# Six of sixteen products with B of a state-space scan moved from VectorE to GpSimd, each released by a node's row-maxima scores

## The chip, the cores and the metric

One core of a Trainium2 chip runs the whole program. The metric is the device time of one execution in microseconds (us); the time before is the median of three runs.

## What is computed

Sixteen sequences of 128 rows and 256 features go through three stages, each added to or replacing the stream:

```
x = x + mamba(layernorm(x))        # h_t = exp(dt*A) * h_{t-1} + (dt*u) * B_t ;  y_t = sum_n h_t[n] * C_t[n]
x = x + mlstm(layernorm(x), ctx)   # four heads, gates, normalised heads
x = x + ffn(layernorm(x))          # six nodes, each: q, k, v projections, softmax attention of 8 heads, Wo, + q
```

In the first stage the state has 512 channels times 16 components per sequence. `(dt*u) * B` is the inflow of the scan; it is the product that the change is about.

## The kernel before

The sequences are taken in eight groups of two (`NG`, `GB`). All engines walk one list, `ORDER`: every step of every stage has a slot in it, a group's FFN (`"f"`) has 67 slots, and the steps of the scan (`"u"`), of its input part (`"a"`) and of the mLSTM (`"x"`) of later groups are put between them by hand-written tables of slots. While the FFN of group g runs, VectorE also does the second half of the scan of group g+1, the mLSTM of group g+1, the input part of group g+2 and the first part of the scan of group g+2. Engines run their own steps strictly in the order of the list and wait for each other on semaphores.

The scan of a group is cut into sixteen units k (`UNITS`), each a tile of 128 partitions by 1024 values in one of three ring buffers (`ring`, unit k in buffer `(16*i+k) % 3`). A unit goes through five steps: ScalarE makes the decays (`dec`, L844, four activations); VectorE makes the inflow, `feed` (L1064): ring = dtus * bs, the product with B; VectorE runs the recurrence in place, `scan` (L1071); VectorE multiplies with C, `weigh` (L1080); TensorE folds the components together, `add` (L535), which frees the buffer (semaphore `ysum`). In the list `feed` of unit k+1 stands ahead of `scan` of unit k. After four units `gather` (L1088, L1090) closes a channel block.

In the FFN each node c (0 to 5) does: q, k and v projections (L632, L613, L642); the scores of all eight heads into a four-bank PSUM tile `heads` (L663, semaphore `smax_ps`); the row maxima of these by VectorE into `mx` (L1171, step `("f","max",c)`); a transpose of `mx` (L668) and the scores again with the maxima taken off (L671, L676); the exponentials (ScalarE L917); values and denominators (L688, L690); the division in two halves by VectorE (L1180, step `attend`); the output projection (L710). "Row maxima" below means L1171, and "ready" the end of the L663 in front of it. The first tensor that L710 needs is the first half of `aT`, its last four matmuls need the second half.

Until the change GpSimd clears some buffers at the start and issues a few transfers; then it has nothing to do. The SyncE queue fills `bs`, `cs`, `dts`, `dtus`, and waits there for the semaphores `inflow` (products done) and `outflow`.

Of the kernel before, what the change touches and what calls it, by code (L numbers as in the profile page):

```python
# [7 lines left out]
ALU = mybir.AluOpType  # L8
# [3 lines left out]
P = 128  # L12
B, L, H = 16, 128, 256
GB = 2
T = GB * L
NG = B // GB
# [21 lines left out]
RING = 3  # L38
STEPS = GB * HC


# [72 lines left out]
for _rank, (_name, _steps, _at, _shift) in enumerate(AT):  # L114
# [7 lines left out]
        -236, -227, -227, -194, -155, -146, -82]  # L122
ORDER += [(at, 5, 0, n, step) for n, (step, at) in enumerate(zip(W_STEPS, W_AT))]
ORDER = [(step, g) for _, _, g, _, step in sorted(ORDER)]

# [39 lines left out]

PRE = ["c0_tail", "dt_c0", "dtu_c0", "pool_warm", "dt_first", "dtu_first", "stats_seen", "in_loaded", "alog_loaded", "win_loaded", "wing_loaded", "wx_loaded", "const_loaded", "pool_consts", "pool_zeros", "vec_consts", "prep_ps", "prep_read",
       "prep_vec", "prep_bias_ps", "prep_bias", "w_loaded", "w_used", "setup_act", "gate_sum"]


def build(nc, x, ctx_in, consts, vecs, rowvecs, w_in, w_x, w_dt, w_out, w_gate, w_edge, w_edgeT, w_node, out):  # L170
    bc_rows = nc.dram_tensor("bc_rows", (2, 2, NS, T), F32, kind="Internal").ap()
    dt_rows = nc.dram_tensor("dt_rows", (2, 2, IC, SD, BLKS, T), F32, kind="Internal").ap()
    with ExitStack() as es:
# [110 lines left out]
        def after(eng, name, i, n):  # L284

            value = i * PER[name] + n
            if value > 0:
                eng.wait_ge(sig[name], value)

        def walk(steps):  # L290

            for (kind, name, n), group in ORDER:
                if kind + name in steps:
                    steps[kind + name](group, n)
# [31 lines left out]
        def _(sp):  # L326
# [62 lines left out]
            def spread_rows(i, q):  # L389

                after(sp, "bc_stored", i, 32)
                for j, (dst, name, used) in enumerate(((bs, "bs_in", "inflow"), (cs, "cs_in", "outflow"))):
                    after(sp, used, i - 1, UNITS - CUNITS + q + 1)
                    rows_of = bc_rows[i % 2, j].rearrange("(n g) t -> g n t", g=NGRP)[q]
                    sp.dma_start(dst[:, q, :], rows_of.partition_broadcast(SD)
                                 ).then_inc(sig[f"{name}{q}"], 16)

            def chunk(i, c):
                if i == 0 and c == 0:
                    return  # L400

                for j, (dst, name, used) in enumerate(((dts, "dt", "decay"), (dtus, "dtu", "inflow"))):
                    after(sp, f"{name}_stored", i, 16 * BLKS)
                    after(sp, used, i, (c - 1) * CUNITS)
                    sp.dma_start(dst[c % 2][:].rearrange("p k t -> p (k t)"),
# [544 lines left out]
        def _(dve):  # L950
# [103 lines left out]
            def feed(i, k):  # L1054

                c, q = k // CUNITS, k % CUNITS
                if q == 0:
                    if i == 0 and c == 0:
                        dve.wait_ge(sig["dtu_first"], 16 * BLKS)
                    after(dve, f"dtu_in{c % 2}", i, 16 * (c // 2 + c % 2))  # L1060
                if c == 0:
                    after(dve, f"bs_in{q}", i, 16)
                after(dve, "ysum", i, k - RING + 1)
# [3 lines left out]
            def scan(i, k):  # L1067
                states = ring[(i * UNITS + k) % RING][:].rearrange("p k t -> p (k t)")
                after(dve, "decay", i, k + 1)
                after(dve, "inflow", i, k + 1)  # L1070
                v.tensor_tensor_scan(states, dec[k % 2][:].rearrange("p k b t -> p (k b t)"), states, 0.0, ALU.mult,  # L1071
# [63 lines left out]
            def head_norm(i, _):  # L1135
# [20 lines left out]
                scale = rowv[:, 0:1, :].rearrange("p o (h d) -> p o h d", h=XH)  # L1156
                m_chain.link(v.tensor_tensor(hb, hb, scale.broadcast_to([P, GB, XH, XD]), ALU.mult))

            def mlstm_out(i, step):
                if step == 1:  # L1160
                    return
                xi = xr[i % 2]
                heads_of = xi[:].rearrange("p b (h d) -> p b h d", h=XH)
# [50 lines left out]
        def _(pool):  # L1214
# [15 lines left out]
            first_chunk(pool, dtus, dtu, "dtu")  # L1230


# [63 lines left out]
```

## Time and profile before

| | |
|---|---|
| three runs | 1228.12, 1223.46 and 1228.3 us; median 1228.12 |
| profiled execution | span 1224.7 us, first to last instruction; no time of its own is listed, and the median stands 3.4 us above this span |
| TensorE | busy 1102.9 us, 90% of the span |
| VectorE | busy 980.0 us, 80% |
| ScalarE | busy 733.8 us, 60% |
| GpSimd | busy 15.2 us, all before 47 us |
| mean granted TensorE clock | 0.939 of full speed |

The page gives busy time per engine, the groups of instructions with the idle time in front of them and what ended it, and the chain of work that ended last. The timeline gives single instructions, and in square brackets how long the engine was idle before one and which instruction released it. An instruction on VectorE can be shown to start up to 0.1 us before the end of the one before.

### The profile page before, as it was taken

To read this page: it belongs to the slowest core of one execution; us is meant where nothing else is said; L and a number is where in the kernel's file an instruction comes from. 1 tells how busy PE (TensorE), PEld (TensorE's weight loads), DVE (VectorE), ACT (ScalarE), POOL (GpSimd) and SP (SyncE) were. 2 spreads that over 40 slices of the span, in tenths; PEclk is the share of its full clock that TensorE was granted. 3 is DMA by queue.
4 is the path that set the end of the run, shared out by engine and by line. 5 is a ranking of instruction groups with operands and counts; after the bars stand their busy time and mean duration, and the time that the engine had idled before them with its cause. 6 is when DMAs were issued, how large, how long until landed. Compare 5 with 4: busy or idle time off the path is not lost.

```text
span 1224.7 us, 27095 instructions
## 1 busy us (share of the span) xinstructions
PE 1102.9 (90%) x11540; PEld 842.8 (69%) x11540; DVE 980.0 (80%) x1219; ACT 733.8 (60%) x1728; POOL 15.2 (1%) x32
## 2 busy tenths in 40 slices
PE   8866779999999998999899989999999988998886
PEld 6743456767777676777677767777777766776775
DVE  2398978799998998999999989999988989635122
ACT  3535442776577665776587657765676656544443
POOL 4000000000000000000000000000000000000000
PEclk9777686999999999999999999999999999999998
DMA  6631523013110412041112201041104120000000
GB/s 203 204 115 58 161 93 120 36 36 106 44 62 11 131 36 70 7 134 36 36 37 82 86 17 61 17 124 45 52 11 131 35 62 1 2 2 10 2 1 10
DMA packets 52791, 76.08 MB, mean 62 GB/s; under 512 B 13696, under 2 KB 37504, under 8 KB 52672
## 3 DMA queue, kind: packets, MB, share of 16 engines
q1 hardware_dynamic: 51968, 73.81, 19.2%
q8 instruction: 90, 1.47, 0.5%
q0 software_dynamic: 704, 0.56, 0.2%
q14 instruction: 29, 0.24, 0.1%
HBM read 62.55 MB, written 10.75 MB: 60 GB/s over the span
## 4 chain that ended last, share of the span: by engine, by line
PE 62%; DVE 10%; ACT 8%; issue 3%; DVEq 0%; ACTq 0%
PE ps L632 7%; PE heads L642 7%; PE ps L710 6%; PE ps L703 5%; PE ps L613 5%; PE heads L663 4%; PE heads L671 4%; PE ps L535 4%; PE ps L502 3%; DVE mx L1171 3%; PE ps L559 2%; PE ps L688 2%; PE heads L688 1%; PE heads L613 1%; PE ps L690 1%
## 5 line engine op out<-in xcount | busy, mean ns | idle before, releaser
L1071 DVE TENSOR_TENSOR_SCAN ring<-dec,ring 128x1024 f32<-128x1024 f32 x128 | 292.0, 2281 | 1.7 <-ACT dec L844 1.2
L844 ACT ACTIVATE dec<-dts,a_neg 128x254 f32<-128x254 f32 x512 | 220.0, 500 | 16.8 <-DVE ring L1071 16.7
L1171 DVE TENSOR_REDUCE mx<-heads 128x16 f32<-128x2048 f32 x48 | 109.7, 2286 | 65.3 <-PE heads L663 64.7
L1080 DVE TENSOR_TENSOR ring<-ring,cs 128x1024 f32<-128x1024 f32 x128 | 156.0, 1218 | 1.9
L1064 DVE TENSOR_TENSOR ring<-dtus,bs 128x1024 f32<-128x1024 f32 x128 | 155.1, 1217 | 2.3 <-PE ps L535 1.8
L917 ACT ACTIVATE pr<-heads 128x512 f32<-128x512 f32 x192 | 99.1, 603 | 41.3 <-PE heads L676 41.3
L535 PE MATMUL ps<-ring,fold 128*32 128x256 f32 x1024 | 88.6, 416 | 26.3 <-DVE ring L1080 26.2
L710 PE MATMUL ps<-aT,wo_f 128*128 128x256 f32 x384 | 94.1, 387 | 8.0 <-DVE aT L1180 8.0
L703 PE MATMUL ps<-node,we_f 128*128 128x256 f32 x384 | 99.2, 403 | 0.0
L632 PE MATMUL ps<-node,wq_f 128*128 128x256 f32 x384 | 94.9, 390 | 3.4 <-ACT node L932 3.4
L642 PE MATMUL heads<-wv_f,node 128*128 128x256 f32 x384 | 94.1, 388 | 0.0
L632 PEld LDWEIGHTS ps<-node,wq_f 128*128 128x128 f32 x384 | 69.8, 190 | 27.2 <-ACT node L932 18.5
L710 PEld LDWEIGHTS ps<-aT,wo_f 128*128 128x128 f32 x384 | 70.1, 190 | 25.5 <-DVE aT L1180 17.2
L613 PE MATMUL ps<-node,wk_f 128*128 128x256 f32 x320 | 83.1, 405 | 0.0
L703 PEld LDWEIGHTS ps<-node,we_f 128*128 128x128 f32 x384 | 74.0, 200 | 13.2 <-issue 2.4
L642 PEld LDWEIGHTS heads<-wv_f,node 128*128 128x128 f32 x384 | 70.4, 190 | 17.3 <-issue 9.1
L897 ACT ACTIVATE qT<-ps,fb 128x256 f32<-128x256 f32 x96 | 40.2, 470 | 56.4 <-PE ps L632 55.4
L663 PE MATMUL heads<-kT,qT 32*128 32x128 f32 x1536 | 57.9, 288 | 16.7 <-ACT qT L897 11.9
L502 PE MATMUL ps<-th,win 128*128 128x256 f32 x256 | 65.4, 401 | 8.0 <-ACT u L777 5.8
L613 PEld LDWEIGHTS ps<-node,wk_f 128*128 128x128 f32 x320 | 60.0, 198 | 18.3 <-issue 9.3
L663 PEld LDWEIGHTS heads<-kT,qT 32*128 32x128 f32 x1536 | 49.5, 190 | 30.0 <-issue 30.0
L932 ACT ACTIVATE node<-ps,fb 128x256 f32<-128x256 f32 x96 | 40.1, 468 | 43.1 <-PE ps L710 43.1
(183 smaller groups left out, 1753.5 us busy)
## 6 DMA issues: line engine op xcount, KB each, us to landing
dts<-dt_rows SPq DMA_DIRECT2D x31, 512.0 KB, 3.9
dtus<-dt_rows SPq DMA_DIRECT2D x31, 512.0 KB, 5.1
node<-in_w_edgeT SPq DMA_DIRECT2D x18, 256.0 KB, 3.1
bs<-bc_rows SPq DMA_DIRECT2D x32, 128.0 KB, 5.0
cs<-bc_rows SPq DMA_DIRECT2D x32, 128.0 KB, 5.1
dt_rows<-dt SPq DMA_DIRECT2D x32, 128.0 KB, 2.4
dt_rows<-th SPq DMA_DIRECT2D x32, 128.0 KB, 2.5
xin<-in_x SPq DMA_DIRECT2D x8, 256.0 KB, 3.1
```

The costliest lines, as they stand in the source:

```text
L535: last = mm(MY[SD * blk:SD * (blk + 1), 0:T], fold[:], ring[(i * UNITS + k) % RING][:, blk, :], start=(q == 0), stop=(q == NGRP - 1), tile ...
L613: last = mm(bank[:, a * T:(a + 1) * T], w[:, k, a * P:(a + 1) * P], src[:, k, :], start=(k == 0), stop=(k == HC - 1))
L632: last = mm(FA[:, a * T:(a + 1) * T], wq_f[c][:, k, a * P:(a + 1) * P], src[:, k, :], start=(a == 0 and k == 0), stop=(k == HC - 1), skip_ ...
L642: last = mm(X3[:, b * H:(b + 1) * H], node[SLOT[GRAPH[c]["v"]]][:, k, b * L:(b + 1) * L], wv_f[c][:, k, :], start=(k == 0), stop=(k == HC ...
L663: last = mm(heads[:, h, to], qT[at], kT[c % 2][at], start=True, stop=True, tile_position=(FD * h, 0))
L703: mm(ED[:, a * T:(a + 1) * T], we_f[c][:, k, a * P:(a + 1) * P], src[:, k, :], start=(a == 0 and k == 0), stop=False, skip_group_check=True)
L710: last = mm(ED[:, a * T:(a + 1) * T], wo_f[c][:, k, a * P:(a + 1) * P], aT[:, k, :], start=False, stop=(k == HC - 1), skip_group_check=True)
L844: last = fn(dec[k % 2][:, blk, :, 1:L], dts[c % 2][:, blk, :].rearrange("p (b t) -> p b t", b=GB)[:, :, 1:L], ACT.Exp, scale=a_neg[:, c, b ...
L1064: v.tensor_tensor(ring[(i * UNITS + k) % RING][:], dtus[c % 2][:], bs[:, q:q + 1, :].broadcast_to([P, BLKS, T]), ALU.mult).then_inc(sig["i ...
L1071: v.tensor_tensor_scan(states, dec[k % 2][:].rearrange("p k b t -> p (k b t)"), states, 0.0, ALU.mult, ALU.add).then_inc(sig["state"], 1)
L1080: v.tensor_tensor(states[:], states[:], cs[:, q:q + 1, :].broadcast_to([P, BLKS, T]), ALU.mult).then_inc(sig["outflow"], 1)
L1171: v.tensor_reduce(mx[:].rearrange("p (h s) -> p h s", h=HPC)[:, :, 0:STEPS], heads[:].rearrange("p h (s k) -> p h s k", s=STEPS), AX.X, AL ...
```

## The change

`POOL_FED` names, for each group, the units whose product GpSimd makes: none in group 0, units 8, 11 and 14 in group 1, and 2, 4, 6, 8, 11 and 14 in groups 2 to 7, 39 in all. VectorE skips these. GpSimd's new step stands in the list directly behind a row maximum (`POOL_AT`), and waits for the scores of that node (`smax_ps`), for its inputs and for the ring buffer. Its products count in a semaphore of their own, `pool_fed`, and whoever waited for the count of products now waits for both (`wait_fed`). Steps of all other engines stay in their slots. Besides, the last product of `head_norm` is only marked, and what reads it waits for it one step later.

```diff
+POOL_FED = ((), (8, 11, 14)) + ((2, 4, 6, 8, 11, 14),) * (NG - 2)
...
+POOL_AT = [(2, -30.95), (4, -19.95), (6, -8.95), (8, 3.05), (11, 14.05), (14, 25.05)]
+ORDER += [(FSLOTS * (g - 1) + at, 6, g, k, ("u", "pfeed", k)) for g in range(1, NG) for k, at in POOL_AT if k in POOL_FED[g]]
...
+        def wait_fed(eng, i, n):
+
+            mine = sum(UNITS - len(POOL_FED[g]) for g in range(i)) + len([k for k in range(n) if k not in POOL_FED[i]])
+            pools = sum(len(POOL_FED[g]) for g in range(i)) + len([k for k in POOL_FED[i] if k < n])
+            if mine:
+                eng.wait_ge(sig["inflow"], mine)
+            if pools:
+                eng.wait_ge(sig["pool_fed"], pools)
...
             def feed(i, k):
 
                 c, q = k // CUNITS, k % CUNITS
-                if q == 0:
-                    if i == 0 and c == 0:
-                        dve.wait_ge(sig["dtu_first"], 16 * BLKS)
-                    after(dve, f"dtu_in{c % 2}", i, 16 * (c // 2 + c % 2))
-                if c == 0:
-                    after(dve, f"bs_in{q}", i, 16)
+                if k in POOL_FED[i]:
+                    return
+                if i == 0 and c == 0:
+                    dve.wait_ge(sig["dtu_first"], 16 * BLKS)
+                after(dve, f"dtu_in{c % 2}", i, 16 * (c // 2 + c % 2))
+                after(dve, f"bs_in{q}", i, 16)
...
             def scan(i, k):
                 states = ring[(i * UNITS + k) % RING][:].rearrange("p k t -> p (k t)")
                 after(dve, "decay", i, k + 1)
-                after(dve, "inflow", i, k + 1)
+                wait_fed(dve, i, k + 1)
...
-                m_chain.link(v.tensor_tensor(hb, hb, scale.broadcast_to([P, GB, XH, XD]), ALU.mult))
+                m_chain.mark(v.tensor_tensor(hb, hb, scale.broadcast_to([P, GB, XH, XD]), ALU.mult))
 
             def mlstm_out(i, step):
                 if step == 1:
                     return
+                m_chain.wait(m_chain.n)
...
+            def feed(i, k):
+
+                c, q = k // CUNITS, k % CUNITS
+                if k not in POOL_FED[i]:
+                    return
+                grp, node_c = [(grp, step[2]) for step, grp in ORDER[:ORDER.index((("u", "pfeed", k), i))]
+                               if step[:2] == ("f", "max")][-1]
+                after(pool, "smax_ps", grp, node_c + 1)
+                after(pool, f"dtu_in{c % 2}", i, 16 * (c // 2 + c % 2))
+                after(pool, f"bs_in{q}", i, 16)
+                after(pool, "ysum", i, k - RING + 1)
+                g.tensor_tensor(ring[(i * UNITS + k) % RING][:], dtus[c % 2][:],
+                                bs[:, q:q + 1, :].broadcast_to([P, BLKS, T]), ALU.mult).then_inc(sig["pool_fed"], 1)
+
+            walk(dict(upfeed=feed))
```

VectorE around the row maxima of node 2 in the FFN of group 3, before: L1064 is `feed`, the two products shown are those of units 14 and 15 of group 4.

```order
L1090 TENSOR_TENSOR gate1<-gate1,u1 128x256
L1080 TENSOR_TENSOR ring2<-ring2,cs 128x1024
L1064 TENSOR_TENSOR ring1<-dtus1,bs 128x1024
L1171 TENSOR_REDUCE mx<-heads 128x4x4
L1071 SCALAR_TENSOR_TENSOR ring0<-dec1,ring0 128x1024
L1047 SCALAR_TENSOR_TENSOR dt<-dt,th 128x1024
L1050 TENSOR_TENSOR th<-dt,u0 128x1024
L1080 TENSOR_TENSOR ring0<-ring0,cs 128x1024
L1064 TENSOR_TENSOR ring2<-dtus1,bs 128x1024
L1071 SCALAR_TENSOR_TENSOR ring1<-dec0,ring1 128x1024
L1180 TENSOR_TENSOR aT<-ps3,aT 128x256
```

The same place after the change; line numbers have moved: `feed` is L1082, `scan` L1089, `weigh` L1098, row maxima L1190, `attend` L1199.

```order
L1108 TENSOR_TENSOR gate1<-gate1,u1 128x256
L1098 TENSOR_TENSOR ring2<-ring2,cs 128x1024
L1190 TENSOR_REDUCE mx<-heads 128x4x4
L1089 SCALAR_TENSOR_TENSOR ring0<-dec1,ring0 128x1024
L1065 SCALAR_TENSOR_TENSOR dt<-dt,th 128x1024
L1068 TENSOR_TENSOR th<-dt,u0 128x1024
L1098 TENSOR_TENSOR ring0<-ring0,cs 128x1024
L1082 TENSOR_TENSOR ring2<-dtus1,bs 128x1024
L1089 SCALAR_TENSOR_TENSOR ring1<-dec0,ring1 128x1024
L1199 TENSOR_TENSOR aT<-ps3,aT 128x256
```

Only the product of unit 14, directly ahead of the row maxima, is gone; everything behind them is as it was.

GpSimd's stream for group 4, units 2, 4, 6, 8, 11 and 14 with their waits (`bs_in` and `dtu_in` are the inputs' transfers); it has nothing else between them:

```order
L1262 TENSOR_TENSOR ring0<-dtus0,bs 128x1024 [waits bs_in2,ysum,dtu_in0,smax_ps]
L1262 TENSOR_TENSOR ring2<-dtus1,bs 128x1024 [waits bs_in0,ysum,dtu_in1,smax_ps]
L1262 TENSOR_TENSOR ring1<-dtus1,bs 128x1024 [waits bs_in2,ysum,dtu_in1,smax_ps]
L1262 TENSOR_TENSOR ring0<-dtus0,bs 128x1024 [waits bs_in0,ysum,dtu_in0,smax_ps]
L1262 TENSOR_TENSOR ring0<-dtus0,bs 128x1024 [waits bs_in3,ysum,dtu_in0,smax_ps]
L1262 TENSOR_TENSOR ring0<-dtus1,bs 128x1024 [waits bs_in2,ysum,dtu_in1,smax_ps]
```

Each is one instruction of 1024 values per partition, and none was on GpSimd before. The first three are behind the scores of nodes 3 to 5 of FFN 2, the last three behind nodes 0 to 2 of FFN 3.

VectorE around the row maxima of node 0 in the FFN of group 6 (units 7 and 8 of group 7), before and then after:

```order
L1064 TENSOR_TENSOR ring2<-dtus1,bs 128x1024 [waits ysum]
L1071 SCALAR_TENSOR_TENSOR ring1<-dec0,ring1 128x1024 [waits inflow,decay]
L1080 TENSOR_TENSOR ring1<-ring1,cs 128x1024 [waits state]
L1064 TENSOR_TENSOR ring0<-dtus0,bs 128x1024 [waits ysum,dtu_in0]
L1171 TENSOR_REDUCE mx<-heads 128x4x4 [waits smax_ps]
L1071 SCALAR_TENSOR_TENSOR ring2<-dec1,ring2 128x1024 [waits inflow,decay]
L1080 TENSOR_TENSOR ring2<-ring2,cs 128x1024 [waits state]
L1064 TENSOR_TENSOR ring1<-dtus0,bs 128x1024 [waits ysum]
L1071 SCALAR_TENSOR_TENSOR ring0<-dec0,ring0 128x1024 [waits inflow,decay]
```

```order
L1082 TENSOR_TENSOR ring2<-dtus1,bs 128x1024 [waits ysum,bs_in3,dtu_in1]
L1089 SCALAR_TENSOR_TENSOR ring1<-dec0,ring1 128x1024 [waits pool_fed,inflow,decay]
L1098 TENSOR_TENSOR ring1<-ring1,cs 128x1024 [waits state]
L1190 TENSOR_REDUCE mx<-heads 128x4x4 [waits smax_ps]
L1089 SCALAR_TENSOR_TENSOR ring2<-dec1,ring2 128x1024 [waits pool_fed,inflow,decay]
L1098 TENSOR_TENSOR ring2<-ring2,cs 128x1024 [waits state]
L1082 TENSOR_TENSOR ring1<-dtus0,bs 128x1024 [waits ysum,bs_in1,dtu_in0]
L1089 SCALAR_TENSOR_TENSOR ring0<-dec0,ring0 128x1024 [waits pool_fed,inflow,decay]
```

The product into `ring0` (unit 8) is gone from in front of the row maxima, and the recurrences now also wait for GpSimd's count.

## Rows read from the trace of the kernel before

**Rows 1.** Busy time of each engine in two stretches (start:end, length, busy, instructions, granted clock).

```profile
590.00:720.00 130.00, 122.58 (x1392) 94.14 (x1391) 120.40 (x147) 89.37 (x213) 0.00 (x0) 0.99 0.19 58
982.00:1102.00 120.00, 108.97 (x1306) 84.07 (x1306) 84.86 (x106) 65.63 (x163) 0.00 (x0) 0.99 0.06 17
```

**Rows 2.** Page, part 5: the product with B on VectorE.

```profile
L1064 DVE TENSOR_TENSOR ring<-dtus,bs 128x1024 f32<-128x1024 f32 x128 | 155.1, 1217 | 2.3 <-PE ps L535 1.8
```

**Rows 3.** GpSimd's instructions, grouped by line and form (busy us, mean ns).

```profile
L1220 POOL MEMSET dec<- 128x1024 f32 x2 | 1.8, 951 | 0.0
...
L1216 POOL MEMSET ones<- 128x128 f32 x1 | 0.2, 204 | 0.3 <-POOLq L1289 0.3
```

**Rows 4.** Timeline of all engines, 43.8 to 45.5 us.

```profile
43.89 0.42 DVE L1045 TENSOR_TENSOR th<-dt,u 128x256 f32<-128x256 f32 x1
...
44.61 1.08 POOL L322 DMA_DIRECT2D dtus<-th  x2 [31.05 <-DVE th L1045]
```

**Rows 5.** Timeline of VectorE, 600 to 735 us (start, length, instruction, idle before).

```profile
629.37 0.42 DVE L1180 TENSOR_TENSOR aT<-ps,aT 128x256 f32<-128x256 f32 x1 [0.95 <-ACT aT L927]
...
648.55 0.41 DVE L1180 TENSOR_TENSOR aT<-heads,aT 128x256 f32<-128x256 f32 x1
...
657.46 2.29 DVE L1171 TENSOR_REDUCE mx<-heads 128x16 f32<-128x2048 f32 x1 [2.07 <-PE heads L663]
659.67 2.28 DVE L1071 TENSOR_TENSOR_SCAN ring<-dec,ring 128x1024 f32<-128x1024 f32 x1
...
670.16 0.42 DVE L1180 TENSOR_TENSOR aT<-heads,aT 128x256 f32<-128x256 f32 x1
...
676.33 2.29 DVE L1171 TENSOR_REDUCE mx<-heads 128x16 f32<-128x2048 f32 x1
...
679.04 0.42 DVE L1090 TENSOR_TENSOR gate<-gate,u 128x256 f32<-128x256 f32 x1
...
684.09 0.69 DVE L1102 TENSOR_TENSOR xr<-xr,ps 128x512 f32<-128x512 f32 x1 [0.15 <-PE ps L559]
```

**Rows 6.** Timeline of TensorE, 600 to 735 us.

```profile
648.17 1.98 PE L710 MATMUL ps<-aT,wo_f 128*128 128x256 f32 x8
...
655.83 1.58 PE L663 MATMUL heads<-kT,qT 32*128 32x128 f32 x32
...
669.99 1.89 PE L710 MATMUL ps<-aT,wo_f 128*128 128x256 f32 x8
...
676.20 0.64 PE L535 MATMUL ps<-ring,fold 128*32 128x256 f32 x8
```

**Rows 7.** Timeline of TensorE, in the groups of 264 us and of 786 us.

```profile
278.19 2.05 PE L710 MATMUL ps<-aT,wo_f 128*128 128x256 f32 x8
...
801.45 1.13 PE L710 MATMUL ps<-aT,wo_f 128*128 128x256 f32 x4 [0.17 <-DVE aT L1180]
```

**Rows 8.** Timeline of VectorE, 264 to 287 us.

```profile
278.63 0.42 DVE L1180 TENSOR_TENSOR aT<-heads,aT 128x256 f32<-128x256 f32 x1
```

**Rows 9.** Timeline of VectorE, 984 to 1060 us.

```profile
1004.28 1.22 DVE L1064 TENSOR_TENSOR ring<-dtus,bs 128x1024 f32<-128x1024 f32 x1
1005.41 2.28 DVE L1171 TENSOR_REDUCE mx<-heads 128x16 f32<-128x2048 f32 x1
```

**Rows 10.** Timeline of TensorE, 984 to 1130 us.

```profile
1003.19 1.18 PE L663 MATMUL heads<-kT,qT 32*128 32x128 f32 x32 [0.73 <-issue]
...
1007.75 0.33 PE L668 MATMUL ps<-cst,mx 128*128 128x128 f32 x1 [0.77 <-DVE mx L1171]
...
1015.71 1.99 PE L710 MATMUL ps<-aT,wo_f 128*128 128x256 f32 x8 [1.99 <-DVE aT L1180]
...
1043.51 0.33 PE L668 MATMUL ps<-cst,mx 128*128 128x128 f32 x1 [0.63 <-DVE mx L1171]
...
1126.20 0.33 PE L668 MATMUL ps<-cst,mx 128*128 128x128 f32 x1 [0.48 <-DVE mx L1171]
```

**Rows 11.** Who waited for whom, whole run (us in total, times, longest).

```profile
PE ps L668 <- DVE mx L1171: 6.2, 8, 2.4
```

More of the change, by code:

```diff
@@ L164 @@
 )
-PRE = ["c0_tail", "dt_c0", "dtu_c0", "pool_warm", "dt_first", "dtu_first", "stats_seen", "in_loaded", "alog_loaded", "win_loaded", "wing_loaded", "wx_loaded", "const_loaded", "pool_consts", "pool_zeros", "vec_consts", "prep_ps", "prep_read",
+PRE = ["pool_fed", "c0_tail", "dt_c0", "dtu_c0", "pool_warm", "dt_first", "dtu_first", "stats_seen", "in_loaded", "alog_loaded", "win_loaded", "wing_loaded", "wx_loaded", "const_loaded", "pool_consts", "pool_zeros", "vec_consts", "prep_ps", "prep_read",
        "prep_vec", "prep_bias_ps", "prep_bias", "w_loaded", "w_used", "setup_act", "gate_sum"]
@@ L391, in spread_rows @@
                 after(sp, "bc_stored", i, 32)
-                for j, (dst, name, used) in enumerate(((bs, "bs_in", "inflow"), (cs, "cs_in", "outflow"))):
-                    after(sp, used, i - 1, UNITS - CUNITS + q + 1)
+                for j, (dst, name) in enumerate(((bs, "bs_in"), (cs, "cs_in"))):
+                    if j:
+                        after(sp, "outflow", i - 1, UNITS - CUNITS + q + 1)
+                    elif i:
+                        wait_fed(sp, i - 1, UNITS - CUNITS + q + 1)
                     rows_of = bc_rows[i % 2, j].rearrange("(n g) t -> g n t", g=NGRP)[q]
@@ L400, in chunk @@
                     return
-                for j, (dst, name, used) in enumerate(((dts, "dt", "decay"), (dtus, "dtu", "inflow"))):
+                for j, (dst, name) in enumerate(((dts, "dt"), (dtus, "dtu"))):
                     after(sp, f"{name}_stored", i, 16 * BLKS)
-                    after(sp, used, i, (c - 1) * CUNITS)
+                    if j:
+                        wait_fed(sp, i - (c < 1), (c - 1) * CUNITS if c else UNITS - CUNITS)
+                    else:
+                        after(sp, "decay", i, (c - 1) * CUNITS)
                     sp.dma_start(dst[c % 2][:].rearrange("p k t -> p (k t)"),
```

## The prediction

> **What bounds the kernel now.** I began with the busy time by stretch. In a middle group TensorE is busy 122.58 of 130 us and VectorE 120.40; in the stretch that holds the last scan steps VectorE has fallen to 84.86 of 120 and TensorE to 108.97 [rows 1]. Both engines look full in the middle, so the busy share does not say which one pays. The timelines do. The row maxima of node 2 were preceded by 2.07 us in which VectorE stood idle until the scores were there [rows 5]: VectorE reaches this point early, and what it does ahead of the row maxima is covered. Behind them it is the other way round. It runs without a pause through the recurrence and what follows, and the second half of `aT` is finished when TensorE comes to it, or just after. So a group is a chain of stretches from one node's scores to the next; ahead of the scores VectorE has time to spare, and behind them it has almost none in some nodes. The exception is FFN 6, where the input part of a later group is missing from TensorE's work: there VectorE comes late to two row maxima and TensorE waits for it, 0.77 and 0.63 us at L668 and 1.99 us at L710 [rows 10].
>
> **What is removed.** 39 products of 1.217 us [rows 2], 47.5 us of VectorE's 980. Which of them stood on the path? Units 8, 11 and 14 were made ahead of the row maxima of nodes 0, 1 and 2, unit 6 ahead of node 5, unit 2 between nodes 3 and 4, unit 4 just behind node 4. In FFN 0 to 5 the scores end TensorE's stretch and VectorE is there in time or in the last instruction before, and TensorE does not wait for `mx`. Earlier arrival brings nothing: gain 0. What covers it is TensorE's own work of the stretch; without that cover each would be worth 1.13 us, the distance from one product's start to the next instruction (1004.28 to 1005.41 [rows 9]). In FFN 6 there is a gain:
> - Node 0: scores end at 1003.19 + 1.18 = 1004.37 [rows 10], the row maxima start at 1005.41, behind the product of unit 8 [rows 9]. Without it they start 0.06 after the scores, as at node 2 of group 3 (657.41 to 657.46), so 0.98 earlier. What is behind them, up to the wait of 1.99 us at L710, comes forward by this.
> - Node 1: no gain. Node 2: the product of unit 14 goes, and with it TensorE's 0.63 us [rows 10].
> Together 0.98 + 0.63 = 1.6 us, if nothing is given back.
>
> **What is added: 39 products on GpSimd.** The trace has no elementwise product on GpSimd. Its nearest rows are the clearing of a 128x1024 tile in 0.951 us and of a 128x128 tile in 0.204 [rows 3], 0.83 ns for a value and 0.10 us fixed. A product reads two values and writes one. If the write is hidden behind the reads it takes 2 x 0.83 x 1.024 + 0.10 = 1.81 us; if all three take turns, 2.66. I take the middle, 2.24 us. GpSimd started 0.30 us after the VectorE instruction that released it (43.89 + 0.42 to 44.61 [rows 4]). So a product ends 0.30 + 2.24 = 2.54 us after the scores.
>
> The Trainium skill (GPSIMD Engine Reference, "Performance versus the Vector engine") gives 4497 ns for an addition of 2048 fp32 values and advises VectorE for such work. With the fixed 0.10 us that makes, as an estimate, 2.30 us here, and the total below would be 2.7 us instead of 1.6. No row here shows it.
>
> Is anybody waiting for that end? The users of the products are not: the recurrence that reads unit 8 stands behind the row maxima, another recurrence, a weighing, six convolution steps and another product; unit 11 has two products and recurrences in front of it, and so on. The SyncE queue doesn't either: what refills `bs` behind unit 14 stands in its queue behind a transfer that waits for the weighing of unit 13, which is later. The 39 products cost VectorE only if the two engines are in each other's way when both read operands from SBUF. During the row maxima they are not, since these read PSUM. The instruction behind them (a recurrence) reads two SBUF tensors. No row shows the two at work together. The lower bound of the cost is nothing; the upper bound is that this instruction waits until the product is done. I take the upper bound with the middle product, because it is also near the middle of all combinations. The recurrence stood 659.67 - 657.41 = 2.26 us behind the scores [rows 5, 6]. So the overhang is 2.54 - 2.26 = 0.28 us. What each stretch makes of it, in FFN 0 to 5:
> - Node 0: VectorE waited 0.95 us for ScalarE ahead of `aT` [rows 5]. The overhang disappears: 0.
> - Node 1: the second half of `aT` was done at 648.55 + 0.41 = 648.96 [rows 5]; L710 needs it halfway through, 648.17 + 0.99 = 649.16 [rows 6]. With the 0.04 us from one to the other, 0.16 to spare: cost 0.12, six times, 0.7 us.
> - Node 2: in FFN 0 the half was done at 279.05 [rows 8] and needed at 278.19 + 0.95 = 279.14 [rows 7], 0.05 to spare: 0.23, and I count FFN 1 and 5 like it: 0.69. In FFN 4 TensorE already waited 0.17 us for it [rows 7]: 0.28 in full. In FFN 2 and 3 the half was done at 670.58 [rows 5], needed at 669.99 + 0.95 = 670.94 [rows 6]: 0. Sum 1.0 us.
> - Node 3: unit 2 needs the ring buffer of the unit 15 before, which TensorE frees at 676.20 + 0.64 = 676.84 [rows 6], after the scores. The product ends at 676.84 + 0.30 + 2.24 = 679.38. The next instruction with two SBUF tensors is the gate at 679.04 [rows 5], so 0.34 late; ahead of L1102, where VectorE waited 0.15 [rows 5], 0.19 is left, six times 1.1 us.
> - Nodes 4 and 5: at node 4 VectorE was still in a recurrence when the scores came, is free now, and is ahead by that much; at node 5 nothing with two large SBUF operands follows within reach. 0.
> That is 2.8 us. In FFN 6 the overhang takes 0.28 of the 0.98 at node 0 and 0.12 at node 1; the gain there is 0.70 - 0.12 + 0.63 = 1.2. The moved wait of the mLSTM norm can let `aT` start some 0.08 us earlier, the amount by which the recurrence at 659.67 starts before the row maxima's end [rows 5]; under 1 us in all, and nothing where ScalarE is the later one. I count it 0. More waits stand on VectorE's products and recurrences; they are met long before and are taken up while the instruction ahead runs: 0.
>
> **Sum.** +2.8 - 1.2 = +1.6 us on the profiled execution's 1224.7. Its surroundings, 3.4 us to the median, are the same in both kernels. 1228.12 + 1.6 = 1229.7 us, +0.13%. About 0.5%, 6.1 us, is what a measurement of this kernel can tell from no change.
>
> **Ends.** Nothing given back (a product of 1.81 us, or no hindrance): -1.6, 1226.5 us. A product of 2.66 us makes an overhang of 0.70: node 1 3.2, node 2 1.95 + 0.70 + 0.68 = 3.3, node 3 0.61 x 6 = 3.7, and FFN 6 gains only 0.28 - 0.54 + 0.63 = 0.4: +9.8, 1237.9 us. Between 0.28 and 0.70 each 0.1 us of overhang costs 2.0 us, so 6.1 us is passed at 0.51, a product of 2.47 us.
>
> **Rivals.**
> - *The overhang becomes the bound* (slower): the product takes 2.47 us or more and VectorE stands still behind every row maximum of nodes 1 to 3. For it: node 2 has no time to spare in any view, and the upper bound from the clearing rows allows it. Against it: the middle of the bounds doesn't reach it. 1234 to 1238 us, chance 0.20.
> - *The product catches the operands first* (slower): if GpSimd is released while VectorE still has an instruction with two SBUF operands to start ahead of the row maxima, `mx` itself is 2.24 us later, straight on TensorE's path. Decides from three such meetings a run. Against it: before the change at most one instruction was under way at the scores, and 0.30 us to wake leaves it to finish. Chance 0.04. The Trainium skill (SBUF — State Buffer, "Who interferes with whom") says that a VectorE instruction with two SBUF inputs and a GpSimd instruction that reads SBUF exclude each other for their whole length, by order of issue; by that rule both rivals' mechanism exists, and their price depends on who comes first; no row here shows it.
> - *No hindrance* (the change does its work and nobody needed it): 1226.5 us, chance 0.14.
> - *TensorE's waits for the row maxima vanish as a whole* (faster): 6.2 us over the run, eight waits [rows 11], would give 1221.9 us. Against it: two of the eight are in FFN 6 and counted; others stand in FFN 7 (0.48 at 1126.20 [rows 10]), which has no scan beside it. Chance 0.05.
> - The forecast, overhang 0.1 to 0.5: chance 0.57.
>
> Faster by over 0.5%: 0.06. Within: 0.57 + 0.14 = 0.71 less a little for the sum of small errors, 0.70. Slower: 0.24. The range takes the no-hindrance end and most of the long product, with the scatter of the runs shown (1223.46 to 1228.3) below: 1224 to 1236.5.
>
> **What would show it.** GpSimd's busy time rises to about 39 x 2.24 + 15 = 103 us; a product's length beside the row maxima decides the sum. The start of the recurrence behind the row maxima: 2.26 us after the scores without hindrance, 2.5 by my sum, more in the rival. VectorE's busy time falls by 47 us and its idle time ahead of row maxima grows by about as much. TensorE's 0.77 and 0.63 us at L668 in FFN 6 are gone, the 1.99 at L710 is about 1.3. In FFN 4 the wait of 0.17 us in the middle of L710 becomes 0.45. I am wrong if a product takes far from 2.2 us, if VectorE's other instructions get longer beside it, or if the row maxima do.

## The result: slower by 0.85%

The kernel with the change takes 1237.29 us, the median of 13 runs (1228.36 to 1241.91); the kernel before took 1227.42 us in 13 runs (1221.03 to 1230.5). The ratio is 1.0085, with a 95% interval of 1.0062 to 1.0108, so it is slower, and the whole interval lies above the half per cent that the prediction took as the least difference it could tell. The forecast of 1229.7 us was wrong, and the median lies 0.8 us above the range. The profiled execution took 1241.91 us, its span 1240.1 us, where that of before was 1224.7: 15.4 us to explain. (The median of the runs moved less, 9.9 us; the profiled one is the slowest of the thirteen.) "Kernel 1" to "kernel 7" below mean the kernels of experiments 1 to 7.

The page of the kernel with the change, busy time by engine and two groups of its costliest instructions (busy us, mean ns, then idle time before them and what ended it). Lines have moved by 18 or 19: L1064 is now L1082, L1071 is L1089, L1090 is L1108, L1171 is L1190, L663 is L681.

```profile
PE 1106.7 (89%) x11540; PEld 841.8 (68%) x11540; DVE 950.5 (77%) x1180; ACT 732.6 (59%) x1728; POOL 110.8 (9%) x71
...
L1262 POOL TENSOR_TENSOR ring<-dtus,bs 128x1024 f32<-128x1024 f32 x39 | 95.6, 2450 | 917.4 <-PE heads L681 796.9
...
L1082 DVE TENSOR_TENSOR ring<-dtus,bs 128x1024 f32<-128x1024 f32 x89 | 112.0, 1266 | 2.5 <-PE ps L553 2.0
```

GpSimd does 39 products in 95.6 us, 2450 ns each, and VectorE is left with 89 of 128. But the mean of VectorE's own products, 1217 ns in [rows 2], has risen to 1266: some of them stood still. Next, GpSimd's waits over the whole run (us in total, times, longest), and then the lengths of its products (minimum/median/maximum in ns):

```profile
POOL ring L1262 <- PE heads L681: 796.9, 33, 177.9
POOL ring L1262 <- DMA bs<-bc_rows: 120.5, 6, 21.1
```

The products' line:

```profile
L1262 POOL TENSOR_TENSOR ring<-dtus,bs x39: 2344/2359/3253, 223.5 to 1056.2; 128x1024 f32<-128x1024 f32 x39
```

33 products waited for the scores, as the change intends. Six waited for a transfer of `bs`. One product a group in six groups is exactly unit 2, and this wait is in no term of the prediction.

Where the 15.4 us are is found by the distance from one node's scores to the next, as in the prediction's stretches. From node 3 to node 4 it was 22.77, 23.12, 22.73, 23.09, 22.76 and 22.73 us in FFN 0 to 5; it is 24.70, 26.27, 26.33, 24.67, 24.66 and 26.02. That is 15.45 us more, the whole loss. In FFN 0 to 5 node 0 to 1 stays 21.98, node 4 to 5 stays 20.43, node 1 to 2 goes from 18.97 to 19.03 and node 2 to 3 from 18.76 to 18.83 where the granted clock is 1.00 in both. What else differs goes with that clock (from node 5 of FFN 2 to node 0 of FFN 3 it is 26.57 us at 1.00 before, 28.02 at 0.94 now; behind FFN 0 27.57 at 0.94 before, 26.45 at 1.00 now), up to 1.5 us either way. All the other distances, the start and the end together cancel to 0.05 us in these two executions.

The stretch behind node 3 in FFN 3, first SyncE's queue (a row is a transfer's issue), then GpSimd, VectorE and TensorE, all from timelines of the kernel with the change:

```profile
670.09 2.82 SPq L390 DMA_DIRECT2D dt_rows<-dt  x4
672.95 1.90 SPq L394 DMA_DIRECT2D dt_rows<-th  x4
...
677.70 0.54 SPq L410 DMA_DIRECT2D bs<-bc_rows  x1
...
680.29 0.54 SPq L410 DMA_DIRECT2D bs<-bc_rows  x1
```

GpSimd in the same stretch:

```profile
685.91 2.35 POOL L1262 TENSOR_TENSOR ring<-dtus,bs 128x1024 f32<-128x1024 f32 x1 [19.12 <-DMA bs<-bc_rows]
```

VectorE in the same stretch:

```profile
683.25 2.28 DVE L1190 TENSOR_REDUCE mx<-heads 128x16 f32<-128x2048 f32 x1
...
685.95 2.59 DVE L1108 TENSOR_TENSOR gate<-gate,u 128x256 f32<-128x256 f32 x1
```

TensorE in the same stretch:

```profile
681.98 1.17 PE L681 MATMUL heads<-kT,qT 32*128 32x128 f32 x32 [0.66 <-ACT qT L915]
683.08 0.64 PE L553 MATMUL ps<-ring,fold 128*32 128x256 f32 x8
...
688.69 3.69 PE L577 MATMUL ps<-wout,gate 128*128 128x256 f32 x16 [1.45 <-DVE gate L1108]
...
696.08 0.66 PE L498 MATMUL ps<-cst,hrow 128*128 128x128 f32 x4 [0.47 <-DVE hrow L1023]
```

The scores of node 3 end at 681.98 + 1.17 = 683.15. The ring buffer is free at 683.08 + 0.64 = 683.72, 0.57 us behind the scores, as I had it. But the rows of B that unit 2 reads are issued at 680.29, behind eight stores of `dt` and `dt`*u, the chunk's own loads and the row group before, and the product starts at 685.91, 5.6 us later. By then VectorE has finished the row maxima, which read PSUM, and is at the gate (L1108), which reads two tensors in SBUF. The gate takes 2.59 us where it took 0.42 in [rows 5]: it is stalled for 2.17 us. TensorE waits 1.45 us for it at L577 and 0.47 us for `hrow` later, 1.92 us together. In the kernel before, the same transfer was issued at 673.18, also too late for an early product (the row maxima started at 676.33 [rows 5]), but VectorE made unit 2 only at 688.61. SyncE's queue in the kernel before:

```profile
673.18 0.55 SPq L395 DMA_DIRECT2D bs<-bc_rows  x1
```

And VectorE's timeline there:

```profile
688.61 1.22 DVE L1064 TENSOR_TENSOR ring<-dtus,bs 128x1024 f32<-128x1024 f32 x1
```

In the six groups the product of unit 2 starts 2.79, 4.43, 4.26, 2.76, 4.47 and 3.39 us behind the scores. Whatever VectorE has in hand with two SBUF operands then pays: the gate in FFN 0 and 3, the products of units 0 and 1 in FFN 2 and 5, the first recurrence in FFN 1 and 4. VectorE's timeline in FFN 2 and FFN 4, kernel with the change:

```profile
551.67 4.54 DVE L1082 TENSOR_TENSOR ring<-dtus,bs 128x1024 f32<-128x1024 f32 x2
...
821.54 4.44 DVE L1089 TENSOR_TENSOR_SCAN ring<-dec,ring 128x1024 f32<-128x1024 f32 x1
```

GpSimd's timeline in FFN 4:

```profile
820.59 3.25 POOL L1262 TENSOR_TENSOR ring<-dtus,bs 128x1024 f32<-128x1024 f32 x1 [20.82 <-DMA bs<-bc_rows]
```

The pair of products takes 4.54 us instead of 2.35, the recurrence 4.44 instead of 2.28: 2.19 and 2.16 us, the same stall as at the gate. In FFN 4 GpSimd came while VectorE was in a product with two SBUF operands (until 821.62); its own product is listed with 3.25 us because it waited as well.

The stall costs 1.9 us on the path wherever it falls, and in three of the six stretches 1.3 to 1.6 us more. Windows of the kernel with the change over the stretches of FFN 2 and 3 and over short pieces in FFN 2 (start:end, length, busy time and instructions of TensorE, its weight loads, VectorE, ScalarE and GpSimd, granted clock, DMA share, GB/s):

```profile
548.00:575.00 27.00, 24.71 (x262) 17.44 (x255) 23.50 (x29) 15.72 (x41) 2.40 (x2) 0.94 0.14 53
683.00:708.00 25.00, 22.77 (x249) 16.69 (x243) 23.13 (x29) 15.46 (x40) 2.42 (x2) 1.00 0.12 43
558.00:560.00 2.00, 1.50 (x48) 1.23 (x48) 1.82 (x5) 0.00 (x0) 0.00 (x0) 1.00 0.00 0
560.00:562.00 2.00, 0.53 (x4) 0.42 (x4) 1.49 (x5) 1.10 (x4) 0.00 (x0) 1.00 0.00 0
562.00:564.00 2.00, 2.00 (x27) 0.82 (x26) 2.00 (x2) 1.75 (x5) 0.00 (x0) 0.69 0.00 0
564.00:566.00 2.00, 2.00 (x6) 0.89 (x5) 2.00 (x4) 1.24 (x4) 0.00 (x0) 0.50 0.00 0
```

In FFN 2 the granted clock falls between 562 and 564 us and is 0.50, TensorE's lower level of 1.2 GHz, from 564 to 566. Before it TensorE had been busy only 1.50 and 0.53 us of two stretches of 2 us: it had waited 1.97 us in one piece for `hrow`. In FFN 3 the same 1.9 us are taken in two pieces, 1.45 and 0.47, and the clock stays at 1.00. FFN 4 shows that one piece doesn't always do it: TensorE waits 1.94 us there, and the clock stays at 1.00. TensorE's timeline at the two places:

```profile
561.47 0.66 PE L498 MATMUL ps<-cst,hrow 128*128 128x128 f32 x4 [1.97 <-DVE hrow L1023]
...
829.04 0.66 PE L498 MATMUL ps<-cst,hrow 128*128 128x128 f32 x4 [1.94 <-DVE hrow L1023]
```

So the sum is 6 x 1.92 = 11.5 us of stalls, 4.6 us of low clock, less 0.6 us that FFN 1 and 3 lost in the kernel before and don't now (23.12 and 23.09, where the rest show 22.7 to 22.8: TensorE waited 0.40 us for `hrow` in both): 15.5, where 15.45 was measured.

### The profile page after: what moved, and what is told of

Its sections match the earlier page's. It is cut to its first block and busy times, and to the rows that moved or that the text cites. A ratio compares the mean times of both kernels' runs of the same rounds, so it can differ in the third digit from the quotient of the medians.

```text
span 1240.1 us, 27202 instructions
## 1 busy us (share of the span) xinstructions
PE 1106.7 (89%) x11540; PEld 841.8 (68%) x11540; DVE 950.5 (77%) x1180; ACT 732.6 (59%) x1728; POOL 110.8 (9%) x71
## 5 line engine op out<-in xcount | busy, mean ns | idle before, releaser
L1089 DVE TENSOR_TENSOR_SCAN ring<-dec,ring 128x1024 f32<-128x1024 f32 x128 | 297.8, 2327 | 1.7 <-ACT dec L862 1.1
L1262 POOL TENSOR_TENSOR ring<-dtus,bs 128x1024 f32<-128x1024 f32 x39 | 95.6, 2450 | 917.4 <-PE heads L681 796.9
L1190 DVE TENSOR_REDUCE mx<-heads 128x16 f32<-128x2048 f32 x48 | 109.7, 2286 | 76.3 <-PE heads L681 75.7
L1098 DVE TENSOR_TENSOR ring<-ring,cs 128x1024 f32<-128x1024 f32 x128 | 156.1, 1219 | 1.9
L1082 DVE TENSOR_TENSOR ring<-dtus,bs 128x1024 f32<-128x1024 f32 x89 | 112.0, 1266 | 2.5 <-PE ps L553 2.0
L728 PE MATMUL ps<-aT,wo_f 128*128 128x256 f32 x384 | 96.0, 391 | 10.4 <-DVE aT L1199 10.3
L728 PEld LDWEIGHTS ps<-aT,wo_f 128*128 128x128 f32 x384 | 70.5, 191 | 29.0 <-DVE aT L1199 20.1
L681 PE MATMUL heads<-kT,qT 32*128 32x128 f32 x1536 | 57.0, 284 | 16.7 <-ACT qT L915 12.0
L681 PEld LDWEIGHTS heads<-kT,qT 32*128 32x128 f32 x1536 | 48.7, 187 | 30.0 <-issue 30.0
```

The source lines that it names most:

```text
L681: last = mm(heads[:, h, to], qT[at], kT[c % 2][at], start=True, stop=True, tile_position=(FD * h, 0))
L728: last = mm(ED[:, a * T:(a + 1) * T], wo_f[c][:, k, a * P:(a + 1) * P], aT[:, k, :], start=False, stop=(k == HC - 1), skip_group_check=True)
L1082: v.tensor_tensor(ring[(i * UNITS + k) % RING][:], dtus[c % 2][:], bs[:, q:q + 1, :].broadcast_to([P, BLKS, T]), ALU.mult).then_inc(sig["i ...
L1098: v.tensor_tensor(states[:], states[:], cs[:, q:q + 1, :].broadcast_to([P, BLKS, T]), ALU.mult).then_inc(sig["outflow"], 1)
L1190: v.tensor_reduce(mx[:].rearrange("p (h s) -> p h s", h=HPC)[:, :, 0:STEPS], heads[:].rearrange("p h (s k) -> p h s k", s=STEPS), AX.X, AL ...
```

## Experiments

**1. Is it unit 2?** All products as changed, but unit 2 back on VectorE.

```
-POOL_FED = ((), (8, 11, 14)) + ((2, 4, 6, 8, 11, 14),) * (NG - 2)
+POOL_FED = ((), (8, 11, 14)) + ((4, 6, 8, 11, 14),) * (NG - 2)
```

> The change without unit 2: GpSimd makes 8, 11 and 14 in group 1 and 4, 6, 8, 11 and 14 in groups 2 to 7; VectorE makes unit 2 again. Theory L (unit 2's product starts only when its row of B has landed, 2.7 us or more behind the scores of node 3, and then shuts VectorE out of its next instruction with two SBUF operands): the distance from the scores of node 3 to those of node 4 is 22.7 to 23.1 us again in all six groups, and the time is that of the kernel before or a little less, ratio to before 0.998 to 1.001. Theory O (the overhang behind every row maximum is the cost): unit 2 is one of six, ratio still 1.006 to 1.008.

Measured: 1225.07 us (1223.04 to 1234.34, 12 runs), ratio to the kernel before 0.999 (0.9967 to 1.0014). The distance from node 3 to node 4 is 22.78, 22.77, 22.75, 22.79, 22.78 and 22.74 us. VectorE behind the row maxima of node 3 in FFN 3:

```profile
678.68 0.43 DVE L1108 TENSOR_TENSOR gate<-gate,u 128x256 f32<-128x256 f32 x1
679.02 2.36 DVE L1082 TENSOR_TENSOR ring<-dtus,bs 128x1024 f32<-128x1024 f32 x2
```

The gate is at 0.43 and the two products at 2.36. The loss is gone, and the other 33 products cost nothing that can be measured. Nor does the moved wait of `head_norm`, which this kernel has too.

**2. Is unit 2 enough?** Only unit 2 on GpSimd, in the same six groups.

```
-POOL_FED = ((), (8, 11, 14)) + ((2, 4, 6, 8, 11, 14),) * (NG - 2)
+POOL_FED = ((), ()) + ((2,),) * (NG - 2)
```

> Only unit 2 of groups 2 to 7 on GpSimd, six products in all, all others on VectorE as before. Theory L: nearly the whole loss, ratio to before 1.008 to 1.012. Theory O: a sixth of it, ratio 1.001 to 1.003.

Measured: 1238.33 us (1234.1 to 1243.64, 6 runs), ratio 1.0077 (1.0046 to 1.0108), the whole loss of the change from six of its 39 products, though just under the 1.008 that was expected at least. Distances 24.69, 24.69, 24.68, 24.68, 24.68 and 26.28. Timelines of VectorE and GpSimd in FFN 3, and the windows of FFN 4 and 5:

```profile
681.49 0.42 DVE L1108 TENSOR_TENSOR gate<-gate,u 128x256 f32<-128x256 f32 x1
681.83 4.52 DVE L1082 TENSOR_TENSOR ring<-dtus,bs 128x1024 f32<-128x1024 f32 x2
```

GpSimd:

```profile
682.70 2.57 POOL L1262 TENSOR_TENSOR ring<-dtus,bs 128x1024 f32<-128x1024 f32 x1 [130.30 <-DMA bs<-bc_rows]
```

The windows, with the columns as above:

```profile
811.00:836.00 25.00, 22.73 (x261) 16.77 (x256) 23.12 (x29) 15.39 (x39) 2.44 (x1) 1.00 0.15 57
943.00:970.00 27.00, 24.72 (x256) 17.49 (x251) 23.09 (x27) 15.47 (x40) 3.22 (x1) 0.94 0.14 52
```

Five stretches lose 1.9 us at a clock of 1.00; the sixth loses 3.5, and its clock is 0.94. The five separate the stall, 1.92 us, from the clock, 1.6 us. In kernels 1, 3 and 4, where TensorE has no such wait behind node 3, the clock is 1.00 in all eighteen of these stretches.

**3. Is it the time at which the rows of B land?** All 39 products on GpSimd, as in the change, but on SyncE's queue the second and third of the four row groups of B (the third is the one that unit 2 reads) stand right behind the first, ahead of the stores of `dt`. The main lines of the edit:

```
+                order = [(0, q), (1, q)]
+                if i:
+                    order = {0: [(0, 0), (1, 0), (0, 1), (0, 2)], 1: [(1, 1)], 2: [(1, 2)], 3: [(0, 3), (1, 3)]}[q]
+                for j, r in order:
```

> All 39 products on GpSimd as in the change; in the SyncE queue of groups 1 to 7 the transfers of the second and third row group of B stand right behind the first row group's, ahead of the stores and reads of dt, so that they don't wait for them. Theory L: the product of unit 2 starts 0.6 to 0.8 us behind the scores of node 3 (when TensorE has freed its buffer), ends just behind the start of the gate, and the time falls to that of the kernel before or below, ratio to before 0.998 to 1.002. If instead a product of unit 2 at this place costs its time wherever its transfer lands, or if theory O holds: ratio 1.006 to 1.010.

Measured: 1225.09 us (1222.77 to 1232.15, 12 runs), ratio 0.9986 (0.9961 to 1.0011); every distance from node 3 to 4 is between 22.73 and 22.78. The timelines of GpSimd and VectorE in FFN 3:

```profile
675.50 2.37 POOL L1266 TENSOR_TENSOR ring<-dtus,bs 128x1024 f32<-128x1024 f32 x1 [17.12 <-PE ps L557]
```

VectorE:

```profile
677.54 0.61 DVE L1112 TENSOR_TENSOR gate<-gate,u 128x256 f32<-128x256 f32 x1
```

The product now waits for TensorE to free the ring buffer (L557 is the L535 of before), starts 0.77 us behind the scores and ends at 677.87. The gate takes 0.61 us instead of 0.42: late by 0.19, of which 0.15 disappear in the time that VectorE had ahead of the L1102 of the kernel before (`xr`). Same products, same engine, and the median is 12.2 us below that of the change (the two were measured apart; the ratios, each to the kernel before measured beside it, are 0.9986 and 1.0085, which is the same difference): the cause is the time of the transfer. Against the kernel before it is no gain that can be told from nothing.

**4. What do the two engines exclude each other by?** In place of unit 2's product GpSimd clears the ring buffer three times in a row. Each clearing writes as much as the product, and none reads anything; the inflow of unit 2 is then left out of the result.

```
+                if k == 2:
+                    tile_k = ring[(i * UNITS + k) % RING][:].rearrange("p k t -> p (k t)")
+                    for n in range(2):
+                        g.memset(tile_k, 0.0).then_inc(sig["pool_part"], 1)
...
+                    g.memset(tile_k, 0.0).then_inc(sig["pool_fed"], 1)
+                    return
```

> As the change, with the product of unit 2 replaced by three fills of the same tile with zero, one after the other (about 3 us of GpSimd, released by the same waits): GpSimd writes there and reads nothing, so unit 2's inflow is zero. If GpSimd and VectorE exclude each other only where both read SBUF operands: the gate keeps its 0.42 us and the two products behind it 2.35 us, node 3 to node 4 is 22.7 to 23.1 us, ratio to before 0.998 to 1.002. If any work of GpSimd on SBUF, or the wait for its count, is what holds VectorE: gate or products are stretched as in the change, ratio 1.006 to 1.012.

Measured: 1224.9 us (1221.79 to 1233.1, 12 runs), ratio 0.9971 (0.9951 to 0.9991), a little below the 0.998 to 1.002 that was expected. GpSimd and VectorE in FFN 3:

```profile
676.16 1.96 POOL L1265 MEMSET ring<- 128x1024 f32 x2 [18.87 <-DMA bs<-bc_rows]
678.17 0.95 POOL L1267 MEMSET ring<- 128x1024 f32 x1
```

VectorE:

```profile
676.46 0.42 DVE L1108 TENSOR_TENSOR gate<-gate,u 128x256 f32<-128x256 f32 x1
676.81 2.35 DVE L1082 TENSOR_TENSOR ring<-dtus,bs 128x1024 f32<-128x1024 f32 x2
679.08 2.28 DVE L1089 TENSOR_TENSOR_SCAN ring<-dec,ring 128x1024 f32<-128x1024 f32 x1
```

The clearing runs from 676.16 to 679.12, across the gate and both products up to the start of the recurrence, and they take 0.42, 2.35 and 2.28 us as always. In FFN 2 and 4 the clearing covers the whole recurrence, which takes 2.29. It starts 2.5 to 5.2 us behind the scores in the six groups, as late as the product did (2.8 to 4.5), and what waited for the product's count waits for the clearing's. So it is neither that wait, nor the late start by itself, nor the writes that cost, it is GpSimd's reading while VectorE wants a second operand from SBUF.

**5. What would every product cost in that place?** Kernel 3, with each product released by the end of the row maxima instead of by the scores.

```
-                after(pool, "smax_ps", grp, node_c + 1)
+                after(pool, "smax_read", grp, node_c + 1)
```

> The kernel with early row groups of B, and every one of the 39 products released by the end of the row maxima instead of by the scores, so about 2.3 us later and beside VectorE's instructions with two SBUF operands. Theory L (whoever reads first keeps the other out for its whole length): a recurrence is under way, GpSimd comes in behind it, and VectorE's next instruction with two operands waits some 2.3 us; less what the stretch has to spare that is 1.4 us at node 0, 2.1 at node 1, 2.2 at node 2, 1.9 at node 3, about 1 each at nodes 4 and 5, some 9 us a group and 55 us in all, ratio 1.03 to 1.05. Rival (VectorE always has its next instruction ready and keeps GpSimd waiting, so that only GpSimd pays): ratio 0.998 to 1.003, with products of 5 us and more.

Measured: 1271.98 us (1270.2 to 1274.76, 4 runs), ratio 1.0356 (1.0336 to 1.0376), inside what was expected. Against the distances of kernel 3, node 1 loses 1.9 us and node 2 2.05, near the 2.1 and 2.2 expected; node 3 loses 1.6 where 1.9 was expected, node 0 0.92 where it was 1.4. Node 4 loses nothing, and node 5 nothing but 1.3 us once, in FFN 0, where about 1 each was expected. That is 6.5 us a group and not 9, and 44 us in all and not 55, with three losses in FFN 6 in it. VectorE and GpSimd at node 2:

```profile
686.27 2.28 DVE L1093 TENSOR_TENSOR_SCAN ring<-dec,ring 128x1024 f32<-128x1024 f32 x1
688.47 3.32 DVE L1069 SCALAR_TENSOR_TENSOR dt<-dt,th 128x1024 f32<-128x1024 f32 x1
```

GpSimd:

```profile
686.44 4.27 POOL L1266 TENSOR_TENSOR ring<-dtus,bs 128x1024 f32<-128x1024 f32 x1 [16.68 <-DVE mx L1194]
```

At node 2 the product comes while the recurrence is running, waits for its end and then goes ahead of VectorE's next instruction, whose 3.32 us are 2.1 too many. The row "4.27" holds 1.9 us of waiting: a long product in the profile is not a slow one.

**6. Is node 2 as tight as I said?** Kernel 3, with the product of unit 14, which starts at the scores of node 2, made twice.

```
+                if k == 14:
+                    g.tensor_tensor(ring[(i * UNITS + k) % RING][:], dtus[c % 2][:],
+                                    bs[:, q:q + 1, :].broadcast_to([P, BLKS, T]), ALU.mult).then_inc(sig["pool_part"], 1)
+                    pool.wait_ge(sig["pool_part"], i)
```

> The kernel with early row groups of B, and the product of unit 14 made twice in a row by GpSimd in groups 1 to 7, about 4.8 us instead of 2.35 behind the scores of node 2. Theory L with my claim that VectorE has nothing to spare behind node 2: 2.2 to 2.4 us more from the scores of node 2 to those of node 3 in each of FFN 0 to 5, none in FFN 6, 13 to 15 us in all (more with low-clock intervals), ratio to before 1.010 to 1.013. If there is a microsecond to spare there: ratio 1.004 to 1.007.

Measured: 1236.64 us (1235.04 to 1240.02, 4 runs), ratio 1.007 (1.0049 to 1.0091). The forecast of 1.010 to 1.013 was missed; by its ratio alone the result would belong to the other one, a microsecond to spare (1.004 to 1.007). One part of it is that I had worked from the kernel before and not from kernel 3, whose ratio was 0.9986: between the two ratios are 0.0084, 10.3 us (11.6 between the medians, taken on different chips). The distances decide. The one from node 2 to 3 goes from 18.83 to 20.96 in FFN 3, 2.13 us, and by as much within 0.02 in FFN 0, 1, 2 and 5, which is all of the stall of 2.12. In FFN 4 the two distances around node 2 grow by 4.2 us together at a clock of 0.94 and 0.90, and in FFN 6 the one behind it goes from 17.64 to 18.53, where I had expected nothing. Six stalls and FFN 6 make 13.6 us; why the medians show 2 to 3 us less is open. VectorE, then TensorE at node 2 of FFN 3:

```profile
664.86 2.36 DVE L1093 TENSOR_TENSOR_SCAN ring<-dec,ring 128x1024 f32<-128x1024 f32 x1
667.14 3.31 DVE L1069 SCALAR_TENSOR_TENSOR dt<-dt,th 128x1024 f32<-128x1024 f32 x1
```

TensorE:

```profile
672.90 0.64 PE L557 MATMUL ps<-ring,fold 128*32 128x256 f32 x8 [1.53 <-DVE ring L1102]
...
678.02 1.13 PE L732 MATMUL ps<-aT,wo_f 128*128 128x256 f32 x4 [0.31 <-DVE aT L1203]
```

VectorE is stalled at L1069 (3.31 us against 1.19 below) and TensorE waits for it at L557 and in the middle of L732. Behind node 2 nothing absorbs a stall, in FFN 2 and 3 neither.

**7. Does the queue's order do something by itself?** The kernel before, with the new order of kernel 3 alone.

> The kernel before, all products on VectorE, with only the SyncE queue's new order: control for what that order does alone. Theory L: VectorE makes unit 2 long after its row has landed, so nothing changes, ratio 0.998 to 1.002. If the early transfers bring something of their own, 0.995 or less.

Measured: 1228.19 us (1225.74 to 1230.8, 12 runs), ratio 0.9997 (0.9985 to 1.001). Nothing. Kernel 3 is faster than the change only because a product on GpSimd needs its rows early; VectorE never did.

## Why the prediction was wrong

**The step that failed** is the term of node 3: "unit 2 needs the ring buffer of the unit 15 before, which TensorE frees at 676.20 + 0.64 = 676.84 [rows 6], after the scores. The product ends at 676.84 + 0.30 + 2.24 = 679.38", 0.34 us late at the gate, 0.19 left on the path, six times, 1.1 us. The buffer is free when I said. But I asked of SyncE's queue only who waits for the product's end ("The SyncE queue doesn't either"), and never when the product's own operand arrives. A move to an earlier place needs that question for each operand. The issue of `bs` stood in the trace of before at 673.18 and an issue takes 5.0 us to land in part 6 of its page, which makes 678.2, 1.9 us behind the scores. With a start there the product meets the gate or what follows with its full length, and the same formula, stall less the time VectorE has to spare, gives 2.17 - 0.15 = 2.0 us for each group; measured 1.92, six times 11.5 us in place of 1.1. The mechanism was priced, at a tenth of its size (0.19 us a group), because its start was wrong. Kernels 1 to 3 show it from three sides.

**The stalls alone leave the range.** 11.5 us of stalls and 0.8 at nodes 1 and 2, less 1.4 in FFN 6 and the 0.6 of FFN 1 and 3, make +10.3 on the 1227.42 us of the kernel before: 1237.7, where the median is 1237.29. The 4.6 us of low clock, which no case of the prediction had, belong to the profiled execution, the slowest of the thirteen; the median doesn't need them.

**The overhang at nodes 0 to 2** (+1.7 us forecast) was right in kind and too large. The product's length was nearly right: 2.36 us against 2.24. The estimate worked out from the figure of the Trainium skill (GPSIMD Engine Reference, "Performance versus the Vector engine"), 2.30 us, was nearer, and the trace agrees with it within 3%. But GpSimd starts 0.11 us behind the scores and not 0.30. VectorE, then GpSimd at node 2 of FFN 3, kernel with the change:

```profile
664.38 2.29 DVE L1190 TENSOR_REDUCE mx<-heads 128x16 f32<-128x2048 f32 x1 [2.81 <-PE heads L681]
666.59 2.36 DVE L1089 TENSOR_TENSOR_SCAN ring<-dec,ring 128x1024 f32<-128x1024 f32 x1
668.87 1.19 DVE L1065 SCALAR_TENSOR_TENSOR dt<-dt,th 128x1024 f32<-128x1024 f32 x1
```

GpSimd:

```profile
664.42 2.37 POOL L1262 TENSOR_TENSOR ring<-dtus,bs 128x1024 f32<-128x1024 f32 x1 [16.68 <-PE heads L681]
```

The product ends at 666.79, the recurrence starts at 666.59, 2.28 us behind the scores, and takes 2.36 us instead of 2.28. VectorE loses 0.08 us here, not 0.28; the distances grow by 0.06 at node 1 and 0.07 at node 2, some 0.8 us in all twelve. That TensorE has nothing to spare behind node 2 was right, kernel 6. Node 0: nothing, right. Nodes 4 and 5: nothing, right. The wait of 0.17 us in FFN 4 at L710 did not become 0.45, it is gone. It and the 0.36 us to spare in FFN 2 and 3, which the prediction took for properties of these groups, were read from stretches around node 2 at a granted clock of 0.92 to 0.99. In kernel 7, with the same work at 1.00 in FFN 3 and 4, the eight matmuls take 2.05 us there as in FFN 0, without a wait.

**FFN 6** gained, about as forecast: the row maxima of node 0 start 0.06 us behind the scores. TensorE's timeline there:

```profile
1018.20 1.17 PE L681 MATMUL heads<-kT,qT 32*128 32x128 f32 x32 [0.73 <-issue]
...
1021.83 0.27 PE L686 MATMUL ps<-cst,mx 128*128 128x128 f32 x1
...
1029.79 3.25 PE L728 MATMUL ps<-aT,wo_f 128*128 128x256 f32 x8 [1.99 <-DVE aT L1199]
```

The 0.77 us at L668 are gone (L686 now, 0.27 us, no wait), and those of node 2 as well; what is left of [rows 11], from the waits over the whole run:

```profile
PE ps L686 <- DVE mx L1190: 4.8, 6, 2.4
```

The forecast for FFN 6 was 1.2 us; kernel 1 shows 19.53 - 18.62 = 0.91 from node 0 to 1 and 18.19 - 17.64 = 0.55 from node 2 to 3, less 0.05 between, 1.4. L710 began 1015.71 - 1004.37 = 11.34 us behind the scores of node 0 and now, as L728, 1029.79 - 1019.37 = 10.42 us: earlier by 0.92, where the forecast was 0.98 less an overhang of 0.28. Its wait did not shrink to 1.3 all the same, since TensorE comes there earlier too. In the profiled execution of the change L728 then takes 3.25 us at a lower clock, and the distance to node 1 is 20.17 at a granted clock of 0.92: the gain of node 0 isn't there. It is in kernels 1 and 3, 18.62 and 18.61 at 1.00.

**VectorE's busy time** fell by 29.5 us, from 980.0 to 950.5, and not by 47. The 39 products are gone. Of the 18 us between, 14.5 are what its other products, the recurrences and the gates were stretched while they stood still. The other 3.4 are that instructions in a row overlap by 0.09 us in the profile, so that a product adds 1.13 us to the busy time and not 1.217. GpSimd's time is 110.8 us and not 103, for the same reason and for products of 2.36 us. I had named longer instructions of VectorE as a sign of being wrong, and they are how the loss shows on the page.

**The rivals.** "The overhang becomes the bound" came nearest in its time, 1234 to 1238 us, and has the right mechanism (VectorE stands still behind the row maxima). Its condition, a product of 2.47 us or more, was not met, and nodes 1 and 2 cost 0.07 us each: the late start at node 3 did it, so that its time fits by luck. "No hindrance" is the state of kernels 1 and 3 within what can be measured. "Catches the operands first" does not happen ahead of the row maxima, which took at most 2.29 us each; at node 3 it is what happens to the second product, the gate or the recurrence. The exclusion itself is as the Trainium skill has it (SBUF — State Buffer, "Who interferes with whom"): VectorE with two SBUF inputs against a GpSimd instruction that reads SBUF, not against one that only writes. The runs agree, with 0.42 us at the gate beside the clearing (kernel 4) and 2.59 beside the product.

## What to carry to other kernels

When work moves to another engine or to an earlier place, find for each operand when it lands and not only who waits for the result; a transfer that came early enough for the old place may be the new start. Between two engines that exclude each other, the instruction's place in time counted more than its length here: 2.36 us beside a reader of PSUM cost 0.07, the same length 2.7 us later cost 1.9. And the mean of a group that rises (1217 to 1266 ns), or a minimum and maximum apart (2344 and 3253), was a stall here and not a slower instruction. A slack of some tenths read from one execution can be the clock of that execution.

## What was not expected of the hardware

- An instruction of VectorE can be shown as started while it still waits for GpSimd, and its end follows that of the product by less than its own length. The gate ended at 685.95 + 2.59 = 688.54, 0.42 us after 688.12, and the product ended at 685.91 + 2.35 = 688.26: if it takes its usual 0.42 us, it did its work from 0.14 us ahead of the end that is shown for the product. In kernel 6 the same sum gives 0.11 (667.14 + 3.31 - 1.19 = 669.26 against 665.15 + 4.22 = 669.37). An overhang of 0.20 us that cost 0.08 at node 2 fits this.
- Where both wait, GpSimd goes between two instructions of VectorE that follow each other directly: the pair of products in kernel 2 takes 4.52 us with GpSimd's 2.57 in it, and in kernel 5 L1069 waits though VectorE was busy until then.
- A single wait of TensorE of 1.94 to 1.97 us was followed by the lower clock in FFN 1, 2 and 5 and not in FFN 4 (in kernel 2, which has five such waits, in FFN 5 alone). It cost 1.3 to 1.6 us each time; what decides between them stays open.
